# First key stack by chunks, another order of the last quarters, and an order of parts for each of 52 steps

## The reference

```python
def reference(x, ctx, Wq, Wk, Wv, Wo, bo, w_gate, w_up, w_down):
    t = layernorm(x)
    Q, K, V = heads(t @ Wq), heads(ctx @ Wk), heads(ctx @ Wv)
    attn = softmax(Q @ K.T * 16 ** -0.5)
    x = x + join_heads(attn @ V) @ Wo + bo
    t = layernorm(x)
    lin = lambda a, w: fp4(a) @ fp4(w).T          # blocks of 16 columns
    return x + lin(silu(lin(t, w_gate)) * lin(t, w_up), w_down)
```

## Time and profile before

| | us |
|---|---|
| median of 3 runs | 3379.75 |
| profiled execution | 3376.89 |
| its span | 3375.1 |
| PE busy | 3209.6 (95%) |
| VectorE (DVE) busy | 2698.0 (80%) |
| ScalarE (ACT) busy | 2282.7 (68%) |
| GpSimd (POOL) busy | 1097.4 (33%) |
| mean granted PE clock | 0.965 |

### The profile page before, as it was taken

One profiled execution on the slowest core, in us unless ns is written; L12 is line 12 of the kernel. 1 busy time (PEld: TensorE's weight loads), 2 busy tenths in 40 slices (PEclk: granted clock), 3 DMA queues, 4 the chain that ended last, 5 costly groups with the idle time before them and its releaser, 6 DMA issues.

```text
span 3375.1 us, 55778 instructions
## 1 busy us (share of the span) xinstructions
PE 3209.6 (95%) x19606; PEld 1657.6 (49%) x19606; DVE 2698.0 (80%) x6009; ACT 2282.7 (68%) x4692; POOL 1097.4 (33%) x1411
## 2 busy tenths in 40 slices
PE   6899999999999999999999999999999999999996
PEld 4344544545455454544545455454544545454444
DVE  6877788888887878878887888878878888887855
ACT  2666677676766767767676776767767677766761
POOL 0213333243333333324343333333333333332332
PEclk6998999999999999999999999999999999999987
DMA  3332133232222322133232222322133232222200
GB/s 78 71 54 47 36 60 56 35 65 39 52 48 40 66 45 50 36 59 58 35 65 35 51 53 42 64 45 53 35 58 56 35 66 43 46 48 46 41 14 8
DMA packets 120783, 163.29 MB, mean 48 GB/s; under 512 B 47125, under 2 KB 93606, under 8 KB 120506
## 3 DMA queue, kind: packets, MB, share of 16 engines
q1 hardware_dynamic: 120506, 159.73, 27.0%
HBM read 46.22 MB, written 8.39 MB: 16 GB/s over the span
## 4 chain that ended last, share of the span: by engine, by line
PE 72%; DVE 11%; ACT 4%; SPq 4%; DMA 4%; POOL 2%; issue 2%; POOLq 0%; DVEq 0%; ACTq 0%
PE out_ps L1014 17%; PE ring L1001 14%; PE ring L1027 13%; PE ring L964 8%; DVE piece_max L1369 6%; PE ring L975 5%; PE ring L931 3%; PE ring L939 3%; DMA k_stack<-k_parts 2%; ACT probs L1140 2%; SPq L820 2%; PE ring L920 2%; DMA q_stack<-neg_rows 2%; PE ring L955 2%; PE ring L949 1%
## 5 line engine op out<-in xcount | busy, mean ns | idle before, releaser
L1369 DVE TENSOR_REDUCE piece_max<-ring 128x1 f32<-128x402 f32 x4096 | 2072.4, 567 | 454.3 <-PE ring L1027 443.5
L1140 ACT ACTIVATE probs<-ring 128x512 f32<-128x512 f32 (+1 forms) x3328 | 1774.8, 605 | 560.4 <-PE ring L1001 544.5
L1014 PE MATMUL out_ps<-probs,v_ones 128*17 128x512 f32 x6656 | 898.9, 612 | 0.8 <-ACT probs L1140 0.8
L1001 PE MATMUL ring<-q_stack,k_stack 50*128 50x512 f32 (+1 forms) x3328 | 841.3, 469 | 37.2 <-DMA q_stack<-neg_rows 24.7
L1027 PE MATMUL ring<-k_stack,q_stack 48*128 48x402 f32 x4096 | 818.9, 391 | 44.8 <-DMA k_stack<-k_parts 32.9
L1001 PEld LDWEIGHTS ring<-q_stack,k_stack 50*128 50x128 f32 (+1 forms) x3328 | 349.5, 184 | 815.4 <-issue 262.0
L1027 PEld LDWEIGHTS ring<-k_stack,q_stack 48*128 48x128 f32 x4096 | 448.6, 192 | 307.9 <-DVE piece_max L1369 95.7
L964 PE MATMUL ring<-wgu_T,xq_T 128*128 128x512 f32 (+1 forms) x1080 | 252.5, 382 | 1.9 <-POOL xq_T L1474 0.5
L1418 POOL TENSOR_TENSOR h<-h,h_grid 128x704 f32<-128x704 f32 (+1 forms) x68 | 101.6, 1494 | 460.2 <-DVE h_grid L1203 460.2
L964 PEld LDWEIGHTS ring<-wgu_T,xq_T 128*128 128x128 f32 x1080 | 192.7, 188 | 53.2 <-issue 22.8
L1014 PEld LDWEIGHTS out_ps<-probs,v_ones 128*17 128x17 f32 x6656 | 110.7, 95 | 218.6 <-issue 183.5
(11 more groups left out here) (170 smaller groups left out, 2662.6 us busy)
## 6 DMA issues: line engine op xcount, KB each, us to landing
k_stack<-k_parts SPq DMA_DIRECT2D x256, 200.1 KB, 4.7
k_stack<-k_parts SPq DMA_DIRECT2D x256, 100.1 KB, 4.3
ctx_in<-in_ctx SPq DMA_DIRECT2D x47, 384.0 KB, 4.0
q_stack<-q_parts SPq DMA_DIRECT2D x256, 64.0 KB, 2.3
x_in<-in_x SPq DMA_DIRECT2D x16, 512.0 KB, 5.5
q_stack<-q_parts SPq DMA_DIRECT2D x256, 32.0 KB, 2.0
resid<-in_x SPq DMA_DIRECT2D x62, 128.0 KB, 2.7
out<-x SPq DMA_DIRECT2D x62, 128.0 KB, 1.8
```

The lines of the kernel that those rows point to most:

```text
L1001: pe.matmul(ring[0:r, bank(kind, batch, item), :], k_stack[rows, at, m * P:m * P + r], q_stack[rows, at, :], start=True, stop=True).then_i ...
L1014: last = pe.matmul(out_ps[32 * j:32 * j + V1, :], v_ones[0:r, batch % 2, m, PER_GROUP * g + j, :], probs[0:r, prob_slot(batch, step, j), : ...
L1140: act.activation(probs[0:r, prob_slot(batch, step, j), :], ring[0:r, at, :], ACT.Exp, scale=SCORE_SCALE).then_inc(probs_ready, 1)
L1369: dve.tensor_reduce(piece_max[:, g % 2, 2 * u + half, t, c:c + 1], ring[:, at, 0:PW], AX_X, ALU.max).then_inc(pieces_max, 1)
```

## The change

The first stack's queries are issued as soon as the first query projection is split, and its keys are issued for each chunk of 512 keys as soon as that chunk is split, with semaphores of their own. The pieces of the first group go through the keys first (all pairs of heads and queries for one quarter of the keys), and begin at the event `("stack_k", 1)`. Early pieces are four pairs, and stand behind the first maxima. `TAIL_AT` and the tables of the body have other numbers, VectorE rounds h of the last quarter alone, and each of the 52 steps picks one of 18 orders. Some index functions are cached on the host, which changes no instruction.

```diff
 POST_AT = [
-    [5, 9, 12, 13, 14, 16, 19, 21, 22, 22, 22, 26, 30, 31, 39, 39, 40],
-    [20, 22, 22, 24, 32, 36, 40, 43, 48, 48, 48, 48, 49, 52, 60, 62, 65],
-    [54, 57, 57, 58, 58, 60, 64, 66, 66, 66, 67, 67, 68, 74, 80, 80, 97],
-    [65, 67, 68, 75, 79, 81, 85, 86, 86, 86, 88, 91, 96, 96, 100, 101, 103],
+    [6, 9, 12, 13, 14, 16, 19, 21, 22, 22, 22, 26, 30, 31, 39, 39, 40],
+    [20, 22, 22, 24, 32, 37, 40, 43, 48, 48, 48, 48, 49, 52, 60, 62, 65],
+    [54, 57, 57, 58, 58, 60, 64, 66, 66, 66, 67, 69, 69, 74, 80, 80, 97],
+    [64, 67, 68, 75, 79, 80, 84, 86, 86, 86, 91, 92, 92, 96, 100, 101, 103],
 ]
 TAIL_AT = [
-    [0, 2, 2, 2, 2, 2, 5, 5, 5, 7, 7, 7, 7, 9, 13, 13, 15],
-    [0, 4, 4, 4, 5, 6, 7, 8, 8, 9, 9, 11, 11, 12, 19, 21, 23],
-    [0, 4, 7, 7, 8, 9, 16, 16, 17, 17, 17, 19, 20, 20, 23, 26, 26],
-    [9, 9, 9, 12, 13, 14, 18, 19, 19, 19, 20, 23, 23, 23, 26, 26, 33],
+    [2, 3, 3, 3, 4, 6, 8, 10, 10, 12, 12, 14, 14, 14, 16, 19, 19],
+    [2, 3, 5, 7, 7, 8, 11, 14, 15, 15, 17, 17, 17, 17, 22, 22, 24],
+    [3, 5, 7, 8, 8, 12, 14, 15, 15, 15, 17, 17, 17, 18, 22, 23, 25],
+    [6, 7, 8, 11, 14, 14, 16, 20, 20, 20, 20, 21, 22, 22, 25, 25, 33],
 ]
-PRE_AT = [24, 27, 27, 30, 45, 45, 50, 56, 61, 61, 63, 66, 69, 69, 70, 71, 71, 72, 74, 76, 85, 99]
+PRE_AT = [26, 27, 27, 37, 45, 45, 50, 56, 61, 63, 63, 66, 69, 69, 70, 71, 71, 72, 74, 76, 85, 95]
-STACK0_AT = [18, 70]
-LN1 = 8
+STACK0_AT = [18, 68]
+LN1 = 9
 PIECES_AT = [
-    [3, 3, 3, 4, 1, 1, 1, 4, 3, 3, 3, 0, 2],
-    [4, 2, 1, 2, 3, 1, 3, 4, 4, 2, 3, 1, 1],
-    [1, 2, 3, 1, 2, 3, 3, 4, 4, 3, 4, 1, 3],
-    [3, 3, 2, 4, 4, 1, 1, 3, 3, 4, 3, 0, 1],
+    [3, 3, 2, 4, 1, 1, 1, 4, 3, 3, 4, 0, 1],
+    [4, 2, 1, 1, 3, 2, 3, 4, 4, 2, 3, 1, 1],
+    [1, 2, 3, 1, 2, 3, 3, 4, 4, 3, 4, 2, 3],
+    [3, 3, 1, 4, 4, 3, 2, 1, 3, 4, 3, 0, 1],
 ]
-EARLY_PIECES = 3
-STEP_ORDERS = ['P S01 W P S23 P V', 'S01 P W P S23 P V', 'S01 P W S23 P V', 'S01 P W P S23 P V', ...
-               'S01 P W S23 P V', 'S01 P W P S23 P V', 'S01 P P S23 W P V', 'S01 P S23 P V']
+EARLY_PIECES = 4
+ORDERS = [
+    "P S01 W P S23 P V",       # 0
+    "S01 P W P S23 P V",       # 1
+    "S01 P W S23 P V",         # 2
+    "S01 P P S23 W P V",       # 3
+    "S01 P S23 P V",           # 4
+    "S01 P S23 P W V",         # 5
+    "S01 P S23 W V P",         # 6
...
+    "S01 P W V S23 P",         # 13
...
+    "S01 w P S23 P W V",       # 17; w: events up to the step's first half
+]
+STEP_ORDERS = [
+    [0, 1, 2, 0, 1, 1, 3, 1, 1, 2, 0, 3, 5],
+    [0, 1, 3, 1, 13, 1, 1, 0, 1, 2, 1, 3, 4],
+    [0, 1, 2, 1, 1, 1, 1, 1, 1, 2, 1, 6, 4],
+    [0, 1, 2, 1, 1, 1, 17, 3, 1, 2, 1, 3, 4],
+]
 LEAD_IN = [
...
-           ("q_proj", 0), ("ones",), ("k_proj", 0, 1), ("ctx_T", 2, 1), ("ctx_T", 3, 0), ("k_proj", 0, 2),
-           ("ctx_T", 3, 1), ("k_proj", 0, 3)]
-VECTOR_ROUNDS = [1, 3]
+           ("q_proj", 0), ("ones",), ("k_proj", 0, 1), ("ctx_T", 2, 1), ("stack_q",), ("stack_k", 0), ("ctx_T", 3, 0),
+           ("k_proj", 0, 2), ("stack_k", 1), ("ctx_T", 3, 1), ("k_proj", 0, 3), ("stack_k", 2), ("stack_k", 3)]
+PIECES_FROM = ("stack_k", 1)
+VECTOR_ROUNDS = [3]
-    def piece_of(n):
+    def piece_of(kind, g, n):
+        if kind == "start" and g == PHASES:
+            return n // (2 * QT) % PAIRS, n // 2 % QT, n // (2 * QT * PAIRS), n % 2
-    PROLOGUE += ([("stack_q",)] + [("stack", 0, u) for u in range(PAIRS)] + [("stack", 1, 0)] + [("bias",), ("prep_v",)]
-                 + [("v_proj", n) for n in range(7)])
-    EARLY = len(PROLOGUE) - 7
+    PROLOGUE += [("stack", 1, 0), ("bias",), ("prep_v",)] + [("v_proj", n) for n in range(7)]
         def spread(group, first, end):
-            many = NPIECE + 2 * EARLY_PIECES
...
+                while n < NPIECE and done * NPIECE >= total * (n + 1):
+                    new.append((("piece", group, n), 0))
...
             put_rounds([("maxima", 0)])
+            for n in range(2 * EARLY_PIECES):
+                put(0, "piece", PHASES + 1, n)
             return seq
...
-            def stack_keys(of, g, u):
+            def stack_keys(of, g, u, a, b, done):
...
+                elif name == "stack_k":
+                    c = event[1]
+                    a, w = chunk(c)
+                    if c < CHUNKS - 1:
+                        sp.wait_ge(split_step, len(VECTOR_SPLITS) + c + 1)
+                    else:
+                        sp.wait_ge(first_split, len(VECTOR_SPLITS))
+                    for u in range(PAIRS):
+                        stack_keys(0, 0, u, a, a + w, first_keys[c] if c < 2 else stacked[pair_slot(0, 0, u)])
...
+                if kind == "start" and g == PHASES:
+                    if u == t == c == half == 0:
+                        pe.wait_ge(first_queries, STACKED)
+                    if u == t == half == 0 and c < 2:
+                        pe.wait_ge(first_keys[c], STACKED)
+                    elif t == half == 0 and c == 2:
+                        pe.wait_ge(stacked[at], STACKED)
+                elif t == c == half == 0:
                     pe.wait_ge(stacked[at], stacked_until(pair(batch, g, u)))
```

More of the change, by code:

```diff
@@ L19 @@
 from contextlib import ExitStack
+from functools import lru_cache
 import concourse.bass as bass
@@ L269, in build @@
         ready = step - (STEPS - VALUES_LEFT)
-        VALUES_LEFT -= min(STEP_ORDERS[step % KEY_TILES].split().count("V"), ready)
+        VALUES_LEFT -= min(ORDERS[STEP_ORDERS[step // KEY_TILES][step % KEY_TILES]].split().count("V"), ready)
     def transposes(event):
@@ L314, in spread @@
                 done += cost
-                while n < many and done * many >= total * (n + 1):
-                    new.append((("piece", group + n // NPIECE, n % NPIECE), 0))
+                while n < NPIECE and done * NPIECE >= total * (n + 1):
+                    new.append((("piece", group, n), 0))
                     n += 1
@@ L321, in sequence @@
         if kind == "start":
-            for n, e in enumerate(PROLOGUE):
-                if n == EARLY:
+            for e in PROLOGUE:
+                if e == PIECES_FROM:
                     first = len(seq)
@@ L353, in sequence @@
                 step = g * KEY_TILES + m
-                left, slots = 2 * PIECES_AT[g][m], STEP_ORDERS[m].count("P")
-                for what in STEP_ORDERS[m].split():
+                parts = ORDERS[STEP_ORDERS[g][m]].split()
+                left, slots = 2 * PIECES_AT[g][m], parts.count("P")
+                for what in parts:
                     if what == "P":
@@ L365, in sequence @@
                             put(NQ, "scores", step, int(j))
-                    elif what == "W":
-                        put_events(2 * step + 1)
+                    elif what in ("w", "W"):
+                        put_events(2 * step + (what == "W"))
                     elif value < step:
@@ L440, in before, with users_before, drains_before @@
         return sum(per(k) for k in at)
+    @lru_cache(None)
+    def users_before(kind, batch, of):
+        return before(kind, batch, lambda k: len(BANK_USERS[k][of]))
+    @lru_cache(None)
+    def drains_before(kind, batch, v):
+        return before(kind, batch, lambda k: DRAINS[k][v])
     def bank(kind, batch, item):
         of = ring_of(kind, item)
-        n = before(kind, batch, lambda k: len(BANK_USERS[k][of])) + FIRST_USE[kind][item]
+        n = users_before(kind, batch, of) + FIRST_USE[kind][item]
         return sum(RINGS[:of]) + n % RINGS[of]
@@ L578, in build @@
         stacked = [sem(f"stacked{i}") for i in range(PAIR_SLOTS)]
+        first_queries = sem("first_queries")
+        first_keys = [sem(f"first_keys{i}") for i in range(2)]
         shift_loaded = [sem(f"shift_loaded{i}") for i in range(2)]
@@ L658, in drained @@
             v = by_vector(kind, event)
-            return (dve_drained if v else act_drained), before(kind, batch, lambda k: DRAINS[k][v]) + DRAIN[kind][event] + 1
+            return (dve_drained if v else act_drained), drains_before(kind, batch, v) + DRAIN[kind][event] + 1
         def ready(kind, batch, event):
@@ L805, in handle @@
                         sp.wait_ge(scores_ready, NSCORES * (ended + 1))
-                    if kind != "start" or g:
-                        stack_queries(of, g, u)
-                    stack_keys(of, g, u)
+                    stack_queries(of, g, u, stacked[pair_slot(of, g, u)])
+                    stack_keys(of, g, u, 0, NK, stacked[pair_slot(of, g, u)])
                 elif name == "stack_q":
@@ L1018, in piece @@
             def piece(kind, batch, g, n):
-                u, t, c, half = piece_of(n)
+                u, t, c, half = piece_of(kind, g, n)
                 at, lo = pair_slot(batch, g, u), HALF * half
-                if t == c == half == 0:
+                if kind == "start" and g == PHASES:
[6 more added lines that the diff above has]
+                elif t == c == half == 0:
                     pe.wait_ge(stacked[at], stacked_until(pair(batch, g, u)))
@@ L1082, in handle @@
```

(5 more changed lines are left out.)

23 lines of the change are left out of this document (16 added, 7 removed).

## The result

The changed kernel takes 3509.21 us (median of 4 runs, 3502.03 to 3512.36). The kernel before took 3379.43 beside it (3378.38 to 3393.36, 4 runs). The ratio is 1.0371, 95% interval 1.034 to 1.0402. I had said 3374, with 3393 as the upper end.

The account below looks back on a forecast made before the run. PE was taken to bound the body (95% busy), with room only at the ends. Start -3.5, body +6.8, clock +3, tail -11 made -4.7 us: 3372 profiled, 3375 against the median, stated as 3374, range 3352 to 3393.

Parts of the forecast that it names:

- the count of pieces through the tables: Body: walking pairs through the step tables gave net +0.45 us a batch, +6.8 us over 15, bounds -6 to +20.
- The wait in the third group: Step 11: the next batch's pair waits about 2.1 us for keys, 0.43 more, with two scores queued behind.
- First group's last step: Body: a pair leaves this step, so the wait for the shift rows grows by 0.38 us a batch.
- Second group, step 4: Body: one pair fewer and an earlier weighted sum should remove the 0.21 us wait for VectorE.
- The other edits: Body: moved transposes, small fp4 steps and other orders, worth -0.15 us a batch, bounds -1 to +1.
- The clock: Body: the longer unbroken wait brings the lower clock to one batch more, +3 us, bounds -15 to +25.
- the body loses what the ends give: Slower rival: clock falls behind second and third groups' ends in nearly every batch, +44 us, total 3413; chance 0.12.
- Start: Up to the first scores: first piece near 32.4, earlier scores, -3.5 us; ends bounded +2 to -10.
- the second rival: Start: pieces fill the shift-row wait, clock holds, 80 to 90 takes 5 to 6 us less; 3360; chance 0.13.
- The pair does not wait: Body rival: the extra pair fills the old gap, -0.4 us a batch instead of +0.4; 3356; chance 0.12.
- Tail: After the last weighted sum: four output quarters step nearly together, -11 us, bounds 0 to -16.
- The tail does not shorten: Tail rival: quarters collide on VectorE in order, 0 gained, about 3386 by the median; chance 0.13.

Follow-up runs that it names:

- Experiment 1: Changed kernel with one pair of pieces of the first group moved back from step 10 to step 12; 3376.23 us, 0.9996 of the kernel before.
- experiment 3: Kernel before with EARLY_PIECES 4 in place of 3 and nothing else; 3575.28 us, 1.0569 of the kernel before.
- experiment 2: Experiment 1 with the third group's extra pair also moved back from step 11 to step 12; 3387.62 us, 1.0007 of the kernel before.
- experiment 4: Changed kernel with the body tables, early count (3) and step orders of before, keeping its new start and tail; 3368.51 us, 0.9971 of the kernel before.
- Experiment 12: The kernel of the three edits with the changed kernel's 52 step orders, except the third group's last step; 3371.57 us, 0.9982 of the kernel before.
- experiment 6: Experiment 4 with VectorE again rounding h of quarter 1 as well as quarter 3; 3368.85 us, 0.9964 of the kernel before.
- three edits: Experiment 4 with the edits of 5, 7 and 8 together; 3317.53 us, 0.9827 of the kernel before.
- 7: Experiment 4 with the third group's last step putting all scores and the weighted sum ahead of the next batch's pieces; 3363.85 us, 0.9942 of the kernel before.
- 8: Experiment 4 with the second group's end transposing the maxima ahead of quarter 1's last gate_up; 3345.6 us, 0.9896 of the kernel before.
- 5: Experiment 4 with bias and v_proj weight split ahead of the start's last key projection, and pieces beginning one chunk later; 3357.15 us, 0.9923 of the kernel before.

## Why the prediction was wrong

**The step that failed** is the body's first one, the count of pieces through the tables. I counted it in the third group and wrote that the pair "comes out of the first group's last step". The same count there reads as follows. With four early pairs, 28 end the group after, and steps 0 to 9 hold 25 of them. Step 10 has four pairs, so its fourth is the first pair of the group behind, whose stack is issued from 2018.93 on. I had it as leaving the last step, and did not look where it went: two steps forward, ahead of its own DMAs. What I priced at +0.38 us was 4.81 us of wait a batch (4.75 in the tenth) and the clock behind it. The whole body was forecast 9.8 us longer with the clock's share, and came out 144.8 longer. Experiment 1 takes that pair away and 133 us go; experiment 3 brings such pairs into the kernel before and 199 us come.

**Point by point.**
- *The wait in the third group:* forecast 2.1 us behind the weighted sum with the scores behind it, measured 2.09 in the tenth batch; over the batches it grew by 0.41 us, for 0.43 forecast. The mechanism and the size were right. Its price was below what experiment 2 can tell.
- *First group's last step:* forecast +0.38 us ahead of the shift rows; measured 1.01 us a batch for 0.35, +0.66. With the pair of step 10 gone (experiment 1) it is back at 0.36.
- *Second group, step 4:* the 0.21 us wait should go; it went (0.24 to 0).
- *The other edits:* -0.15 us a batch forecast, bounds -1 to +1. Open: experiment 1's body is 13.8 us over experiment 4's as it stands, 15.1 under it without the lost time, 6 under it at 0.69 for each us of that. The idle time is alike. Experiment 12 shows that orders and tables belong together: the orders alone cost 54 us.
- *The clock:* I took one batch more at +3 us. The rival "the body loses what the ends give" was right in kind, but its 44 us were reckoned from waits of about 2 us. Here it was 60.5 us of slower work with 84.3 of idle time. The one pair of the first group alone makes 39.3 and 88.1 of these kinds (experiment 1), and the price there needed a wait that I had not seen. The 51 us that I read as the clock's cost before were wrong too: the 14 middle batches take 2831.0 us, which is 42 over 14 clean ones of 199.2.
- *Start:* first piece forecast 32.4, measured 31.77: right. The bulk forecast 37.7, measured 39.58: the key projection waits for a transpose's copy on VectorE (33.37), which stands behind the first piece's reduction, and the split of v_proj's weights (38.69) stands behind three more. The maxima were forecast at 71 and came at 77.36. This delay is 1.9 us of it; pieces and v_proj rounds took 35.8 us (39.58 to 75.37) for 33.5, and VectorE's last reduction ended 2.0 us behind PE's last piece, which I had left out. Start +3.6 us for -3.5. The eight early pieces filled the gap ahead of the first scores, as the second rival has it, but the clock stood at 0.50 from 83 to 91 us as it had at 80 to 90: that rival is out.
- *The pair does not wait,* the last rival, is out too: it waits 2.09 us in the third group and 4.75 in the first.
- *Tail:* -11 forecast, bounds to -16, measured -15.9, the edge of the bounds. The last gate_up was forecast at 3334, 41 us behind the last weighted sum; it came 39.0 behind it. "The tail does not shorten" is out.
- *GpSimd's rounding beside VectorE:* the row 3483.22 of VectorE took 1.82 us while GpSimd rounded, its twin at 3479.23 0.89. The rule of the Trainium skill, "SBUF — State Buffer", section "Who interferes with whom", by which a VectorE instruction with two SBUF inputs and a GpSimd instruction that reads SBUF contend, agrees with this row. But the 4 us by which it would have cut the tail's gain are not there. I had reckoned with five such meetings, 4.5 us. Experiments 4 and 6 differ only in who rounds quarter 1. Against the shortest row of the same shape, VectorE's rows in the tail are lengthened by 6.9 us in all in the one and by 4.3 in the other. So GpSimd's rounding of that quarter costs VectorE 2.6 us, most of it in the rows 3483.22 and 3485.07 here, and VectorE's own rounding of it would cost 3 x 0.89 = 2.7. The two cancel, and the tail of experiment 6 is 0.8 us longer.

```profile
3479.23 0.89 DVE L1243 SCALAR_TENSOR_TENSOR v_ones<-v_ones,k_parts 128x704 f32<-128x704 f32 x1
...
3480.16 0.53 DVE L1259 TENSOR_SCALAR probs<-v_ones 128x704 uint16<-128x704 uint16 x1
...
3485.07 1.59 DVE L1259 TENSOR_SCALAR probs<-v_ones 128x704 uint16<-128x704 uint16 x1
```

## What to carry to other kernels

When a count at the head of a table changes (pieces computed early), walk it through every row of the table, and at each place where a group's last item gives way to the next group's first, ask whether the transfers of that next item are already issued. A wait placed ahead of queued work can cost more than its own length where PE is full: in experiment 1, 88.1 us of idle time and 39.3 of slower work went together. Put the work that is ready ahead of it (scores before the pair, gate_up behind the maxima). And take a moved wait's price from a trace with the granted clock beside it: three edits that gave 11, 5 and 23 us singly gave 51 together, each to within about 10. Last, do not subtract half of the time at the lower clock as if it were all lost: here a us of that was worth 0.69.

## What the runs showed of the hardware

- Half of the time at the lower clock is more than the clock costs. Over 58 runs of the kernel before, 3364.6 to 3403.3 us of span, 1 us of it went with 0.69 us of time.
- The clock's share may not be additive. The lost time was 84.5 us in experiment 4, 79.3 and 69.8 with the repairs of 7 and 8, 86.8 with that of 5, and 37.9 with all three. These are single executions; by the mean clock of all runs, over the whole span, it is 122 us, then 120, 112 and 118, and 84 with all three: 38 less, where the single ones sum to 15.
- Two waits of 0.46 and 0.48 us, after the same matmuls, were followed by a granted clock of 1.00 in one kernel and 0.58 in the other. A wait of 0.47 with the eight pieces of the first behind it was followed by 0.58 as well.
- The eight DMAs of a key and query stack (two each of 64, 32, 200 and 100 KB) took SP 6.2 us to issue in the body (2018.93 to 2025.1), and the piece that waited for them began 3.4 us behind the last issue (2028.48).
